# Two cross-attentions of a Flamingo-style block: split float16 products replaced by float32 products on row halves and column strips of TensorE

## What is computed

```
x = x + tanh(g_xattn[0]) * attention0(layernorm(x), ctx, ctx)      # 8 key heads of 8 channels, 4 query heads for each
x = x + tanh(g_ffn[0])   * experts(layernorm(x), ...)              # 64 experts, the best 8 of each token, and a shared one
x = x + tanh(g_xattn[1]) * (attention1(layernorm(x), ctx, ctx) @ Wc.T + bc)   # 4 key heads of 16 channels, 4 query heads for each
x = x + tanh(g_ffn[1])   * fp8_ffn(layernorm(x), ...)              # 256 -> 1024 -> 256, per-tensor scales
```

## Time and profile before

| | |
|---|---|
| median of 3 runs | 1711.78 us (1705.94 to 1712.32) |
| span of the profiled execution | 1714.7 us |
| TensorE busy | 1178.8 us, 69% |
| VectorE busy | 1084.7 us, 63% |
| GpSimd busy | 883.5 us, 52% |
| ScalarE busy | 783.1 us, 46% |

### The profile page before, as it was taken

One profiled execution on the slowest core, in us unless ns is written; L12 is line 12 of the kernel. 1 busy time (PEld: TensorE's weight loads), 2 busy tenths in 40 slices (PEclk: granted clock), 3 DMA queues, 4 the chain that ended last, 5 costly groups with the idle time before them and its releaser, 6 DMA issues.

```text
span 1714.7 us, 32329 instructions
## 1 busy us (share of the span) xinstructions
PE 1178.8 (69%) x9122; PEld 778.6 (45%) x9132; DVE 1084.7 (63%) x2699; ACT 783.1 (46%) x1599; POOL 883.5 (52%) x846
## 2 busy tenths in 40 slices
PE   4999998133333299999678777871676777846775
PEld 2566665112221266666555555650454444532243
DVE  5899996666666466666444454442765555747898
ACT  3566665122222166666445454441343333433574
POOL 2343343266666633333377777715888888516100
PEclk9999999555555599999777887785788888878878
DMA  9555554032323599999899999984344434100011
GB/s 209 161 151 154 148 154 135 15 115 104 111 106 110 154 281 308 310 301 304 206 242 237 252 246 248 247 199 101 53 54 55 55 55 55 28 1 1 13 37 49
DMA packets 283470, 247.09 MB, mean 144 GB/s; under 512 B 117584, under 2 KB 270032, under 8 KB 282960
## 3 DMA queue, kind: packets, MB, share of 16 engines
q1 hardware_dynamic: 234192, 169.99, 38.9%
q0 software_dynamic: 49152, 75.53, 20.8%
HBM read 111.93 MB, written 117.77 MB: 134 GB/s over the span
## 4 chain that ended last, share of the span: by engine, by line
DMA 24%; DVE 20%; PE 18%; POOL 16%; issue 13%; SPq 4%; ACT 3%; DVEq 1%; POOLq 0%; ACTq 0%
DMA xs<-V 13%; POOL x L632 11%; DMA arena<-xs 8%; PE bank L1493 4%; DVE arena L1318 3%; DMA xs<-arena,V 2%; PE bank L1369 2%; POOL rs L575 2%; PE bank L1381 2%; DVE arena L971 2%; PE bank L1355 2%; PE bank L1569 2%; PE bank L1370 2%; SPq L518 2%; DVE arena L1316 2%
## 5 line engine op out<-in xcount | busy, mean ns | idle before, releaser
L632 POOL DMA_INDIRECT x<-ys,idx x256 | 404.1, 1578 | 129.2 <-issue 57.6
L650 POOL DMA_INDIRECT xs<-V x192 | 187.1, 974 | 207.7 <-DMA xs<-V 188.5
L1493 PE MATMUL bank<-arena,region 128*128 128x128 f16 x2496 | 253.2, 245 | 1.6 <-ACT arena L834 0.9
L834 ACT COPY arena<-bank 128x640 f16<-128x640 f16 x192 | 132.3, 689 | 190.2 <-PE bank L1569 188.2
L1569 PE MATMUL bank<-arena 128*128 128x128 f16 x1440 | 145.2, 240 | 105.3 <-DMA arena<-xs 101.5
L1381 PE MATMUL bank<-arena 128*72 128x256 f32 (+1 forms) x768 | 212.0, 417 | 0.1
L1493 PEld LDWEIGHTS bank<-arena,region 128*128 (+1 forms) x2496 | 187.0, 111 | 19.2 <-issue 6.2
L1569 PEld LDWEIGHTS bank<-arena 128*128 128x128 f16 x1440 | 97.0, 107 | 113.3 <-DMA arena<-xs 85.4
L573 POOL TENSOR_TENSOR ve<-mv,epsilon 128x1 f32<-128x1 f32 x96 | 39.5, 412 | 202.0 <-DVE mv L912 180.0
L1381 PEld LDWEIGHTS bank<-arena 128*72 128x72 f32 (+1 forms) x768 | 117.2, 158 | 46.4 <-issue 13.5
L982 DVE TENSOR_REDUCE arena<-bank 128x8 f32<-128x512 f32 x192 | 124.1, 675 | 15.5 <-PE bank L1355 14.3
(11 more groups left out here) (204 smaller groups left out, 2557.6 us busy)
## 6 DMA issues: line engine op xcount, KB each, us to landing
ys<-arena SPq DMA_DIRECT2D x96, 512.0 KB
arena<-xs SPq DMA_DIRECT2D x288, 160.0 KB
xs<-idx SPq DMA_DIRECT2D x52, 256.0 KB, 2.4
arena<-in_wpairs SPq DMA_DIRECT2D x32, 256.0 KB, 2.6
arena<-in_wpairs SPq DMA_DIRECT2D x128, 64.0 KB, 2.5
x<-ys,idx POOLq DMA_INDIRECT x256, 6.3
out<-arena SPq DMA_DIRECT2D x16, 256.0 KB, 2.2
xs<-idx SPq DMA_DIRECT2D x52, 64.0 KB, 2.1
```

The source lines that it names most:

```text
L632: pool.indirect_dma_start(tile_x(t), None, ys[t // HT], bass.IndirectOffsetOnAxis(ap=idx[:, t, k:k + 1], axis=0), compute_op=ALU.add).then ...
L650: pool.indirect_dma_start(xs[t // HT], bass.IndirectOffsetOnAxis(ap=at_row[:, t, n % 8:n % 8 + 1], axis=0), ROW[t % NROW], None).then_inc( ...
L834: act.copy(XTP[g % 2][q], tpm[n % 2]).then_inc(R_["xt"], 1)
L1493: mm = pe.matmul(o, lhs(a, w, k), rhs(a, w, k), start=(n == 0), stop=(n == 3 * KT - 1))
```

## The change

1. Queries, keys and maxima are float32 and lie in two row halves: rows 0 to 31 hold heads 0 to nk/2-1, rows 32 and on their maxima, rows 64 to 95 the other heads, rows 96 and on theirs. `Q1`, `Q2`, `KD1`, `KD2`, `KH`, `KL` are gone; there are four `Q`, four `XG` and four `KD` of 128 x 2 x 256.
2. VectorE no longer builds the key tables (L971), subtracts the queries (L1028) or normalises twice (L918, L919 become one). SyncE writes each tile's keys from DRAM straight into their diagonal places: `keys(t, layer)`, one DMA for each head (8 a tile in layer 0, 4 in layer 1), each 8 or 16 partitions x 2 runs of 256 bytes. They stand in SyncE's queue ahead of the expert weights of each step. The rows of -1 come by 8 DMAs a layer (`own_rows`); the tables are zeroed first, by VectorE at the start and by GpSimd after attention 0. For layer 1 the 8 + 16 DMAs of the first four tiles are issued in the middle of the experts' stage (g == 48).
3. TensorE: maxima are products of 32 rows x 64 columns (stationary) by 256 (layer 0) or 128 (layer 1) columns in float32, 16 a tile; scores are 64 x 128 by 256 columns in float32, 8 a tile in layer 0 and 4 in layer 1, with no second product added; values are 128 x 32 (layer 0) or 128 x 64 (layer 1) by 256 columns, as many as before, each to its own strip of PSUM partitions instead of adding up. All three transpositions are 128 x 128.
4. The order on TensorE in a step of layer 0 becomes: query transposition of t+2; scores of t, b = 0; maxima of t+1, second half; output transposition of t-1; scores, b = 1; transposition of the maxima of t+1; values, b = 0; values, b = 1; maxima of t+2, first half.
5. In layer 0 the values are written into `VD` by GpSimd (one multiplication by a mask of ones) instead of ScalarE, after it has waited for the value products; ScalarE splits the expert weights at the end of its step instead of its middle. The middle loop holds four steps to a turn.

In the diff below, `first_step` runs on VectorE and `maxima(t, q, gp)`, `scores` and `values` run on TensorE.

```diff
+            def keys(t, layer):
+                nk, d = LAYERS[layer]
+                if t >= NKD:
+                    sp.wait_ge(A[layer]["sc_ready"], (t - NKD + 1) * nk // 2)
+                for k in range(nk):
+                    r, i = k // (nk // 2), k % (nk // 2)
+                    sp.dma_start(KD[t % NKD][r * OWN + i * d:r * OWN + (i + 1) * d, :, i * S:(i + 1) * S],
+                                 ctxT[k * d:(k + 1) * d, 2 * t * S:2 * (t + 1) * S].rearrange("c (b s) -> c b s", b=2)).then_inc(d_kd[t % NKD], 16)
...
-            keys(0)
+            sp.wait_ge(kd_zero, NKD)
+            own_rows(0)
+            for t in range(2):
+                keys(t, 0)
             values(0)
...
             for n in range(2):
                 pair(n, stage[n], d_stage[n])
-            keys(1)
+            for t in range(2, NKD):
+                keys(t, 0)
             sp.dma_start(x[:, 4:12, :], xv[:, 4:12, :]).then_inc(d_x[1], 16)
             values(1)
             sp.dma_start(x[:, 12:NT, :], xv[:, 12:NT, :]).then_inc(d_x[2], 16)
...
             for n in range(2, NPAIR):
+                if n + 2 < NT:
+                    keys(n + 2, 0)
                 sp.wait_ge(wlo_done, 2 * (n - 1))
                 if n > 2:
                     sp.wait_ge(d_w, 80 * (n - 2))
...
+                if g == NG:
+                    sp.wait_ge(kd_zero, 2 * NKD)
+                    own_rows(1)
+                    for t in range(NKD):
+                        keys(t, 1)
...
+                        if past(t, 0):
+                            pool.wait_ge(a["pv_ready"], t + 1)
+                            stand_alone(pool, side_v)
+                        pool.tensor_tensor(VD[j].rearrange("p b (n h w) -> p (b n) h w", h=2, w=P // nk)[:, :, :, 0:d],
+                                           V[:, bass.ds((t + 2) * 2, 2), :].rearrange("p b (n h d) -> p (b n) h d", h=2, d=d),
+                                           ones[:, 0:2].unsqueeze(1).unsqueeze(3).to_broadcast([P, 2 * npair, 2, d]), ALU.mult).then_inc(a["vd_ready"], 1)
...
-                        diagonal(t + 2, KD1[j], KH, 0, a["kd_ready"])
-                        diagonal(t + 2, KD2[j], KL, 1, a["kl_ready"])
...
+                def first_step(t, q):
+                    j = q % 2
                     if inside(t + 1):
...
+                        maxima(t + 1, (q + 1) % NKD, 0)
+                        maxima(t + 1, (q + 1) % NKD, 1)
...
+                        dve.bn_stats(st[:, 1 - j, :], tile_x(t + 3)).then_inc(LNA["stats"], 1)
                     if inside(t - 1):
...
+                        inverse(t - 1)
...
+                        dve.bn_aggr(mv[:, 1 - j, :], st[:, 1 - j, :]).then_inc(LNA["mv"], 1)
+                    if inside(t - 1):
+                        weighted(t - 1, 1 - j)
                     if inside(t + 1):
...
+                        maxima(t + 1, (q + 1) % NKD, 2)
+                        maxima(t + 1, (q + 1) % NKD, 3)
...
                         dve.wait_ge(a["on_ready"], t)
                         dve.scalar_tensor_tensor(tile_x(t - 1), ON[1 - j], tg[:, 0:1], tile_x(t - 1), ALU.mult, ALU.add).then_inc(a["x_done"], 1)
...
+                    if inside(t + 3):
+                        query(t + 3, 1 - j, (q + 3) % NKD)
...
+                def maxima(t, q, gp):
...
+                    for g in range(2 * gpu):
+                        for b in range(2):
+                            for r in range(2):
+                                rows = slice(r * OWN, r * OWN + C // 2)
+                                last[r] = pe.matmul(bank[2 + r][b * S:(b + 1) * S, g * hk * S:(g + 1) * hk * S],
+                                                    Q[q][rows, gp * 2 * gpu + g, b * S:(b + 1) * S], KD[q][rows, b, 0:hk * S],
+                                                    start=True, stop=True)
...
+                def scores(t, q, b):
+                    for p in range(nsc):
+                        for r in range(2):
+                            rows = slice(r * OWN, (r + 1) * OWN)
+                            at = (p if layer == 0 else b) * 256
+                            last[r] = pe.matmul(bank[4 + r][:, at:at + 256], KD[q][rows, b, p * P:(p + 1) * P],
+                                                Q[q][rows, :, b * S:(b + 1) * S], start=True, stop=True)
...
                     for p in range(npair):
-                        mm = pe.matmul(bank[6][0:w, b * 256:(b + 1) * 256], VD[j][:, b, p * w:(p + 1) * w],
-                                       e[:, (p % 2) * 256:(p % 2 + 1) * 256], start=(p == 0), stop=(p == npair - 1))
+                        mm = pe.matmul(bank[6][p * cg:(p + 1) * cg, b * 256:(b + 1) * 256], VD[j][:, b, p * cg:(p + 1) * cg],
+                                       e[:, at:at + 256], start=True, stop=True)
...
                     if inside(t + 1):
                         pe.wait_ge(a["mx_done"], (t + 2) * nmx)
...
-                            mm = pe.transpose(bank[1][0:w, g * P:(g + 1) * P], XG[1 - j][:, g, C:C + w], ident)
+                            mm = pe.transpose(bank[1][:, g * P:(g + 1) * P], XG[(q + 1) % NKD][:, g, :], ident)
                         mm.then_inc(a["t2_ready"], 1)
+                    if inside(t):
+                        values(t, j, 0)
...
                     if inside(t):
                         values(t, j, 1)
+                    if inside(t + 2):
+                        pe.wait_ge(a["q_ready"], t + 3)
+                        pe.wait_ge(d_kd[(q + 2) % NKD], kd_done(t + 2, (q + 2) % NKD, layer))
+                        maxima(t + 2, (q + 2) % NKD, 0)
```

380 lines of the change are left out of this document (170 added, 210 removed).

## The result

The changed kernel takes 1725.6 us (median of 1724.9, 1725.6 and 1726.9), the kernel before 1710.7 (1705.9 to 1712.3, four runs); the ratio is 1.0096 (95% interval 1.0077 to 1.0115). It is slower, as forecast, but by 15 us and not by 109. The profiled executions differ less, 1723.4 us of span against 1714.7; the profile of before is longer than any of its four timed runs.

A forecast was written before the change was run, and what follows sets the result against it. TensorE was taken to bound layer 0, GpSimd attention 1. Layer 0 steps +93, start +5, experts +5 and layer 1 +6 made +109 us on the profiled 1714.7: span 1824, time 1821 us, range 1708 to 1858.

The forecast's parts named there:

- The step that failed: TensorE's tiled float32 products: each moves the queue on by one record, 0.216 us, however many strips; chance 0.48.
- the first rival: TensorE: a waiting record holds back only its own strip, so a tiled group costs 0.99 us; SyncE bounds; chance 0.27.
- The wait at the transposition of the maxima: Layer 0: TensorE waits 1.1 us a step for VectorE's last two reductions, behind a 2.7 us chain.
- the fast rival: Layer 0 with all strips at once: TensorE 6.3 us plus 1.3 us of wait, so the step could be 7.6.
- SyncE.: Layer 0 DMA queue: 5.0 us plus eight key DMAs of 0.47 make 8.8 us a step, hidden under 11.1.
- The point from which the queue decides: SyncE in layer 0: a key DMA issue of 0.39 us separates the two rivals with strips at once.
- Start: Kernel start: zeroing and small DMAs in SyncE's queue delay tile 4's keys until about 60 us; +5 us (0 to 12).
- Experts' stage: 24 issues, some 11 us, between the reload of V and the next fetch; +5 us (0 to 11).
- Layer 1: Attention 1: nothing for 26 steps under GpSimd's 10.9 us; behind the gathers 7.5 against 6.7 us a step, +6 us.
- strips at once, SyncE's issues cheap: Rival: strips run at once and a key DMA issue takes 0.35 us; layer 0 step 7.8, total 1697 us; chance 0.13.
- SyncE takes over: Rival: strips run at once, SyncE's 8.8 us sets layer 0's step; +28, 1740 us (1779 at 0.65 an issue); chance 0.27.
- the rows' halves do not overlap: Rival on TensorE: row halves do not run side by side; layer 0 step 14.7, total 1945 us; chance 0.12.

The follow-up runs named there:

- the experiments with one edit each: Against the changed kernel: second pair of reductions ahead of the reciprocal alone, 1728.5 us; zeroing DMAs moved from layer 0 to routing alone, 1731.1 us.
- all four edits: Changed kernel with reductions ahead of reciprocal, zeroing out of layer 0, layer 1 key DMAs spread, attention 1 scores and second reduction earlier: 1700.8 us on the quieter chip.
- two together: Changed kernel with reductions ahead of the reciprocal and zeroing DMAs moved from layer 0 to routing: 1701.2 us in one run, 1714.0 in a repeat.

## Why the prediction was wrong, point by point

**What bounds the kernel** was read rightly: TensorE in layer 0, GpSimd in attention 1 until the last gather.

**The step that failed** is "the product behind it, though its own strip is free, stands behind that waiting record". From the pairs of the maxima I read that products start in the order issued; but these pairs can't tell an order issued from a strip that is busy, since each third one needs the first one's columns. A group of 8 maxima was put at 2.07 us and takes 1.02, the values 2.07 and 1.00, four scores 1.20 and 1.07. TensorE's sum was 10.0 us and is 7.0: 31 x 3.0 = 93 us, as much as the whole forecast slow-down of layer 0. The bunches of four, and the same 1.05 us with four records of a strip in a row, refute the rule and support the first rival's "two rounds of four" (0.99). That products pass waiting ones of another strip is shown as long as no more than three wait at one strip. The Trainium skill (TensorE: Matmul & The Clock Gate, Part 3, packing small matmuls) has matmuls start strictly in the order issued, which gives the sum of 10.0; the starts with four and eight records of a strip in a row do not agree. Its other rule, one matmul plus some 4 ns for each further tile, gives as an estimate 4 x (0.216 + 0.012) + 0.12 = 1.03 us for a group of 16 records; the trace agrees with 1.00 to 1.03, its starts being 6 to 7 ns apart.

**The wait at the transposition of the maxima** held: 2.7 us of chain forecast, 2.76 measured, the releaser the second pair of reductions, 1.04 us of wait against 1.1 forecast. With the reductions ahead of the reciprocal it is gone. That the wait's size fits is in part luck: of TensorE's work beside the chain, the transposition was put too low (0.45, measured 0.59) and the scores too high (1.20, measured some 1.1), and the two errors cancel.

**Transpositions** cost 0.58, not 0.45 to 0.49 (they are full-width now, 128 x 128 three times): 0.36 us a step. It is a small term, but it is more than half of what lifts the fast rival's TensorE sum from 6.3 to 7.0; the five tiled groups at 1.00 to 1.1 us instead of 0.99 are the rest. Its 6.3 + 1.3 = 7.6 measured 7.0 + 1.04 = 8.04.

**VectorE** lost what was said (39.54 to 22.92 us in the window); that it is worth nothing by itself no run tests; ScalarE waits for nothing new, and GpSimd's longer product is 0.40 us (forecast 0.3 to 0.5).

**SyncE.** 8.8 us a step forecast, 7.95 measured in a quiet turn and 8.1 in the mean: a key DMA takes 0.35 to 0.42 us in the steps, not 0.47. The point from which the queue decides (0.39 us) was a good one: the queue and the loop stood within 0.1 us of each other, and the experiments with one edit each ran into the other bound.

**Start.** +5 forecast, and the first addition came at 44.5 us against 44.9. The first three distances even became 6.3 us shorter, which the prediction did not have; its step of before, 250.9 / 31, spread them over all steps. The keys of tile 4 were issued by 45.6 us, not by 60, for the large V load ahead of them took 7.4 us of issue instead of the 15.35 of the earlier trace rows.

**Experts' stage.** +5 forecast, +4.5 in the one profile. The experiments show some 8 us for the block (a median of 311.5 against 303.1 us from its first issue to the last down product): the mechanism is right, and the size lies within the stated 0 to 11.

**Layer 1.** +6 forecast behind the last gather, +10.3 measured. The last eight distances between additions are 8.2, 8.2, 8.2, 8.4, 8.3, 6.1, 6.1 and 13.6 us, together 66.9; before 6.7, 7.3, 6.7, 6.7, 5.7, 4.9, 4.2 and 14.6, together 56.6. TensorE's work in a step is 8.36 - 1.30 = 7.06 us, under my 7.5; the 1.30 us of waits I had not looked for: 0.64 for ScalarE's copy ahead of the query transposition, which moved to the front of the step, 0.26 for the second reduction, 0.40 for exponentials. While gathers run the pace is 21.5 us for two tiles in both kernels (forecast 2 x 10.9), but for the changed kernel's stretches at half clock, with steps of 12.2 and 13.4 us. The prediction had no term for the clock; a remainder of +2.8 up to the last gather may be theirs, which no run isolates.

Of the rivals, "strips at once, SyncE's issues cheap" had both prices about right (0.99 against 1.02, and 0.35) and gave 1697. Its step of 7.8 us (set by SyncE) was 0.24 too short, but its sum for layer 0, -9, is near the measured -8.4, by luck: those are for the most part the first three distances. It missed the experts' wait (+4.5 in the profile) and the end of layer 1, where it had 6 us gained and 10.3 were lost. "SyncE takes over" gave 1740. The time lies between them. That the rows' halves do not overlap is refuted.

**Beats both:** the kernel with all four edits, 13.7 us under before on one chip (0.9924, 0.99 to 0.9948); its layer 0 is bound by TensorE's own work, 7.16 us a step.

## What to carry to other kernels

Before pricing tiled products by an order of starts, find rows in which order and occupied strip would differ; where there are none, the cheap and the dear case deserve like chances. Where an edit removes one bound, work out the next one to a tenth of a microsecond, and by its mean, not by a quiet turn: here loop, issuing queue and TensorE's work stood at 8.04, 8.1 and 7.16 us, and single edits gave nothing in layer 0 while two together gave 26 us. A block of small DMAs in front of a prefetch, 10.8 us of issues, cost some 8 us here, even three groups ahead; put one into each gap instead. Before two medians are read as the price of an edit, compare the profiles stage by stage, with the granted clock: here nearly half of one gain stood in a stage that the edit had not touched.

## What the runs showed of the hardware that was not expected

- Two-record float32 products in four strips run side by side: 16 records of 0.216 us in 1.0 us (a row half of 32 by a column half of 64, and column strips of 32).
- Records start out of the order issued: with eight of one strip in a row the next strip starts only when the fifth does, so up to three wait without holding back another strip, and four do; 32 records of 0.108 us then take 2.49 us instead of 1.03.
- The time to issue a DMA depends on what stands ahead of it: eight key DMAs take 2.8 us in a quiet step, and 3.8 to 4.6 behind four zeroing DMAs of double size; a single one takes 0.29 to 3.8 us.
- In attention 1 of the changed kernel the granted clock falls to 0.5 for up to 30.7 us, in one case within a wait of 3.94 us of TensorE; a step then takes 13.4 us instead of 8.2 to 8.4.
- Two chips differ by 20 us in the median of the same kernel before (1714.5 and 1734.7); ratios hold only within one chip, and not fully there.
